# The dense stage of a two-layer kernel in batches of two steps: one power, one variance and one set of logits a batch

## The reference, cut

```python
# layer 0
c = lora(x, language) + embedding[language]
xq = act_fake_quant(c)                       # one scale over all of c
h = silu(xq @ Wgq.T) * (xq @ Wuq.T)          # 704 wide
x1 = x + act_fake_quant(h) @ Wdq.T           # one scale over all of h
# layer 1
a = relu(x1 @ W1[lang] + b1[lang]) @ W2[lang] + b2[lang]
z = x1 + a
n = (z - mean(z)) * rsqrt(var(z) + 1e-5) * gamma[lang] + beta[lang]
logits = n @ Wr                              # 9 experts
p = softmax(logits); w, e = top_k(p, 2); w = w / sum(w)
out = x1 + sum over the token's two experts of w * (silu(n @ Wg[e]) * (n @ Wu[e])) @ Wd[e]
```

## Time and profile before

| | us |
|---|---|
| median of 3 runs | 671.34 (667.01, 671.34, 673.58) |
| the profiled execution | 666.66 |
| its span | 664.9 |
| TensorE busy in the span | 604.4 (91%) |
| VectorE busy | 510.1 (77%) |
| ScalarE busy | 442.2 (67%) |
| GpSimd busy | 370.6 (56%) |
| mean granted clock of TensorE | 0.969 |

### The profile page before, as it was taken

The page is one execution under the profiler, slowest core; times in us unless marked ns, Lnnn a source line. Parts: engine busy times, 40 slices in busy tenths (PEclk is TensorE's granted clock), DMA queues, the critical chain, the costliest instruction groups (busy, mean ns, idle before and its releaser), DMA issues.

```text
span 664.9 us, 16051 instructions
## 1 busy us (share of the span) xinstructions
PE 604.4 (91%) x4404; PEld 412.9 (62%) x4404; DVE 510.1 (77%) x1373; ACT 442.2 (67%) x744; POOL 370.6 (56%) x573
## 2 busy tenths in 40 slices
PE   7988888898985558999999999999999999999994
PEld 2243335676663235777777777777777777777773
DVE  5589995688876879888988888888776666666652
ACT  3657995888864556888877787787665444445542
POOL 4014660047767683666657666667666555555544
PEclk9987999999998879999999999999999999999998
DMA  8524001256557649989899889866775556667552
GB/s 268 199 57 128 1 0 49 83 152 212 197 163 252 186 159 192 235 171 202 182 200 173 189 165 189 182 140 114 158 156 110 112 112 104 119 110 110 101 90 32
DMA packets 157300, 95.67 MB, mean 144 GB/s; under 512 B 107924, under 2 KB 150436, under 8 KB 157220
## 3 DMA queue, kind: packets, MB, share of 16 engines
q1 hardware_dynamic: 142900, 76.12, 47.7%
q0 software_dynamic: 13696, 18.51, 15.8%
q10 hardware_dynamic: 624, 0.03, 0.1%
HBM read 44.72 MB, written 24.68 MB: 104 GB/s over the span
## 4 chain that ended last, share of the span: by engine, by line
PE 55%; DVE 16%; issue 11%; POOL 6%; ACT 4%; DMA 3%; SPq 2%; another core or an unknown queue 1%; POOLq 1%; DVEq 0%; ACTq 0%
PE ps L692 29%; PE ps L743 15%; POOL rows L1643 3%; PE ps L564 2%; DVE big L1524 2%; PE ps L671 2%; DVE big L1364 2%; PE ps L803 1%; DMA small<-small 1%; DVE small L1189 1%; PE ps L582 1%; POOL small L1636 1%; PE ps L559 1%; DMA big<-in_low 1%
## 5 line engine op out<-in xcount | busy, mean ns | idle before, releaser
L692 PE MATMUL ps<-big,small 128*128 x1608 | 251.8, 313 | 2.8 <-ACT big L966 1.4
L692 PEld LDWEIGHTS ps<-big,small 128*128 128x128 f16 x1608 | 157.0, 98 | 81.3 <-issue 4.9
L1681 POOL DMA_INDIRECT out<-small x67 | 110.4, 1648 | 137.7 <-DVE small L1489 131.3
L743 PE MATMUL ps<-big,small 128*128 x1105 | 131.4, 273 | 0.5 <-DMA small<-small 0.5
L743 PEld LDWEIGHTS ps<-big,small 128*128 128x128 f16 x1105 | 105.3, 98 | 12.0 <-issue 0.6
L972 ACT ACTIVATE small<-small 128x704 f16<-128x704 f32 x67 | 52.6, 785 | 77.5 <-DVE small L1464 76.9
L1480 DVE SCALAR_TENSOR_TENSOR small<-small 128x64 f16<-128x64 f32 (+1 forms) x134 | 72.6, 583 | 19.9 <-ACT small L976 19.9
L1464 DVE SCALAR_TENSOR_TENSOR small<-ps,small 128x704 f32<-128x704 f32 x67 | 63.5, 948 | 24.9 <-PE ps L692 23.1
L976 ACT ACTIVATE small<-small 128x704 f16<-128x704 f32 x67 | 59.1, 882 | 28.0 <-DVE small L1474 28.0
L1643 POOL DMA_INDIRECT rows<-small x64 | 66.8, 1044 | 18.0 <-issue 18.0
L1654 POOL TENSOR_SCALAR small<-small 128x1 f32<-128x1 f32 x67 | 71.2, 1063 | 0.0
(11 more groups left out here) (256 smaller groups left out, 1048.7 us busy)
## 6 DMA issues: line engine op xcount, KB each, us to landing
small<-rows SPq DMA_DIRECT2D x67, 130.0 KB
big<-in_Wg SPq DMA_DIRECT2D x8, 704.0 KB, 4.6
big<-in_Wu SPq DMA_DIRECT2D x8, 704.0 KB
big<-in_Wd SPq DMA_DIRECT2D x8, 640.0 KB, 5.1
big<-in_xT SPq DMA_DIRECT2D x8, 512.0 KB, 7.1
small<-in_xT SPq DMA_DIRECT2D x16, 256.0 KB
out<-big SPq DMA_DIRECT2D x16, 256.0 KB
rows<-small SPq DMA_DIRECT2D x13, 130.0 KB, 4.2
```

The source lines that it names most:

```text
L692: m = e.matmul(ps[:, 2 * j + h, 0:352], xsT_(t)[:, 2 * xp + k, :], bigh[:, bass.ds(o + (4 * j + 2 * wp + k) * I + 352 * h, 352)], start=(n ...
L743: m = e.matmul(ps[:, 7, 0:H], hTE_(t)[:, hc_, :], bigh[:, bass.ds(o + 8 * I + (6 * wp + c) * H, H)], start=(n == 0), stop=(n == len(terms) ...
L1681: e.indirect_dma_start(out=out[:, :], out_offset=bass.IndirectOffsetOnAxis(ap=tok_(t), axis=0), in_=yw_(t), in_offset=None, compute_op=ALU ...
```

## The change

Every engine's loop over steps becomes a loop over batches, with two steps in a round, in a new order.

- `variance`, `power` and `logits` run once a batch on both steps; `mhalf`, `vpe`, `ssq` are used four columns wide, `rstd` has two buffers.
- `route` is cut in two functions, `first_choice` (up to `df`) and `second_choice`; a `clip_h` stands between.
- TensorE: the filler ahead of `rank` and inside `logits_and_rows` goes; three fillers stand ahead of each `adapter_in`. `adapter_out` of a batch's second step and the `rank` of two batches back stand between the dense products of the batch. `adapter_in` stands ahead of `logits_and_rows`.
- ScalarE: `relu` ahead of `evac_x1`, `squares` at the ends of a round.
- GpSimd: power, then all eight scatters of the batch two back.
- The residual waits for `px` too, as `logits_and_rows` now comes later than `adapter_in`.
- SP: `load_l1` stands behind the x load of its batch's first step; two stores of x1 come after the first two pieces of weights.
- VectorE: `order_experts` and `first_tiles` in the last round, between `residual(15)` and `logits` of batch 6. Behind the stage the last batches' work is ordered anew, and TensorE's `rank(last)` comes ahead of tile 0.

```diff
--- before.py
+++ after.py
@@ carving
-        mhalf = carve(small, a, [2])
+        mhalf = carve(small, a, [2, 2])
...
-        rstd = carve(small, a, [2, 2])
+        rstd = [carve(small, a, [2, 2]) for _ in range(2)]
@@ new helpers
+        def step(of, s):
+            if 0 <= s < ST:
+                of(s)
+
+        def batch(of, b):
+            if 0 <= b < NB:
+                of(b)
@@ sync
-            for i in range(2, 17):
-                if i < ST:
-                    load_xk(i)
+            for i in range(2, ST):
+                load_xk(i)
+                if i >= 6 and i % 2 == 0:
+                    load_l1(i // 2)
                 store_x1(i - 2)
-                b = (i - 5) // 2 + 3
-                if i >= 5 and i % 2 == 1 and b < NB:
-                    load_l1(b)
             load_piece(0)
             load_piece(1)
+            store_x1(ST - 2)
             store_x1(ST - 1)
@@ tensor, rank and logits_and_rows
-                if b < last:
-                    keep_busy(3, 6)
...
-                keep_busy(4 if s else 6, 2 + 2 * (s % 2))
@@ tensor, the stage
-            for i in range(1, 17):
-                if i == 2:
-                    dense_down(1)
-                if i >= 2:
-                    logits_and_rows(i - 2)
-                    adapter_in(i - 2)
-                if i <= ST and i != 2:
-                    dense_down(i - 1)
-                if i >= 2:
-                    adapter_out(i - 2)
-                if i >= 5 and i % 2 == 1:
-                    rank((i - 5) // 2)
-            logits_and_rows(ST - 1)
-            adapter_in(ST - 1)
-            adapter_out(ST - 1)
-            rank(6)
+            for b in range(NB + 1):
+                step(dense_down, 2 * b)
+                batch(rank, b - 2)
+                step(adapter_out, 2 * b - 1)
+                if 0 < b < NB:
+                    keep_busy(3, 1)
+                step(adapter_in, 2 * b)
+                step(dense_down, 2 * b + 1)
+                step(logits_and_rows, 2 * b)
+                if b < NB:
+                    keep_busy(3, 0)
+                step(adapter_in, 2 * b + 1)
+                step(logits_and_rows, 2 * b + 1)
+                step(adapter_out, 2 * b)
+            keep_busy(12, 0)
             piece_top(0)
+            keep_busy(6, 0)
             piece_top(1)
-            keep_busy(14, 0)
+            keep_busy(10, 0)
+            rank(last)
             turn_rows(0)
             proj(0, 0)
             proj(0, 1)
             turn_rows(1)
             piece_top(2)
-            rank(last)
@@ scalar, the stage
-            for i in range(18):
-                if i >= 4:
-                    squares(i - 4)
-                if i < ST:
-                    shift_h(i)
-                if i >= 2:
-                    evac_x1(i - 2)
-                    relu(i - 2)
-                if i % 2 == 1 and i < ST:
-                    adapter_gate(i // 2)
-                if EARLY <= i < ST:
-                    floor_h(i)
-                if i % 2 == 0 and 2 <= i < ST + 2:
-                    scale_beta(i // 2 - 1)
-                if i >= 5 and i % 2 == 1:
-                    second_weight((i - 5) // 2)
-            squares(ST - 2)
+            for b in range(-1, NB + 1):
+                step(squares, 2 * b - 1)
+                batch(second_weight, b - 2)
+                step(shift_h, 2 * b + 2)
+                step(relu, 2 * b)
+                if b >= 0:
+                    step(floor_h, 2 * b + 2)
+                batch(adapter_gate, b)
+                step(evac_x1, 2 * b)
+                step(relu, 2 * b + 1)
+                batch(scale_beta, b - 1)
+                step(shift_h, 2 * b + 3)
+                step(evac_x1, 2 * b + 1)
+                if b >= 0:
+                    step(floor_h, 2 * b + 3)
+                step(squares, 2 * b)
             piece_sum(0)
             piece_sum(1)
             piece_hi(0)
-            squares(ST - 1)
             x_hi(0)
+            second_weight(last)
@@ vector: residual, variance, route
+                w.wait_ge("px", s - 1)
...
-            def variance(s):
+            def variance(b):
+                w.wait_ge("sq", 2 * b + 2)
+                w.wait_ge("rstd", b)
+                e.tensor_scalar(vpe, ssq, eps2[:, 0:1], eps2[:, 1:2], ALU.mult, ALU.add).then_inc(S["vpe"], 1)
...
-            def route(b):
+            def first_choice(b):
...
+            def second_choice(b):
                 e.tensor_tensor(Eq, L2, bc(m2), ALU.is_equal).then_inc(S["rt"], 1)
@@ vector, the stage
-            for i in range(1, 18):
-                rb, odd = divmod(i - 5, 2)
-                if i == 2:
-                    clip_h(1)
-                if i >= 2:
-                    residual(i - 2)
-                if i <= ST and i != 2:
-                    clip_h(i - 1)
-                if i >= 4:
-                    variance(i - 4)
-                if i >= 5 and odd:
-                    positions(rb)
-                if i == 16:
-                    order_experts()
-                    first_tiles()
-                if i >= 3:
-                    gain(i - 3)
-                if i >= 4:
-                    logits(i - 4)
-                    affine(i - 4)
-                if i >= 5:
-                    (payload if odd else route)(rb)
-            variance(ST - 2)
-            positions(6)
-            gain(ST - 1)
-            logits(ST - 2)
-            affine(ST - 2)
-            piece_scale(0)
-            payload(6)
-            variance(ST - 1)
+            for b in range(-1, NB):
+                step(affine, 2 * b - 3)
+                step(residual, 2 * b)
+                step(gain, 2 * b - 1)
+                step(clip_h, 2 * b + 1)
+                batch(positions, b - 2)
+                batch(variance, b - 1)
+                batch(payload, b - 2)
+                step(affine, 2 * b - 4)
+                step(residual, 2 * b + 1)
+                if b == last:
+                    order_experts()
+                    first_tiles()
+                batch(logits, b - 1)
+                batch(first_choice, b - 1)
+                step(clip_h, 2 * b + 2)
+                batch(second_choice, b - 1)
+                step(gain, 2 * b)
+            affine(ST - 3)
+            gain(ST - 1)
+            positions(last - 1)
+            variance(last)
+            payload(last - 1)
+            affine(2 * last - 2)
+            piece_scale(0)
+            logits(last)
+            first_choice(last)
+            second_choice(last)
             piece_scale(1)
             x_lo(0)
             piece_lo(0, (0, 1))
             evac_rows(0)
-            logits(ST - 1)
-            affine(ST - 1)
             piece_lo(1, (0, 1))
             x_lo(1)
-            route(last)
-            piece_scale(2)
+            affine(ST - 1)
             positions(last)
             payload(last)
+            affine(ST - 2)
+            piece_scale(2)
@@ gpsimd
-                e.tensor_tensor(rstd[:, r, :], vpe[:, r, :], mhalf, ALU.pow).then_inc(S["rstd"], 1)
+                e.tensor_tensor(rstd[b % 2], vpe, mhalf, ALU.pow).then_inc(S["rstd"], 1)
...
-                w.wait_ge("aff", 2 * b + half + 1)
+                w.wait_ge("aff", 2 * b + 2 - half)
...
-            for i in range(4, 18):
-                power(i - 4)
-                b, half = divmod(i - 7, 2)
-                if i >= 7:
-                    scatter(b, half)
-            power(ST - 2)
-            scatter(5, 1)
-            power(ST - 1)
-            scatter(6, 0)
-            scatter(6, 1)
-            scatter(last, 0)
-            scatter(last, 1)
+            power(0)
+            for b in range(1, NB + 2):
+                batch(power, b)
+                if b >= 2:
+                    scatter(b - 2, 0)
+                    scatter(b - 2, 1)
```

36 lines of the change are left out of this document (16 added, 20 removed).

## The result

The changed kernel took 683.30 us (median of 4 runs, 682.18 to 687.06) against 670.82 for the kernel before (4 runs): a ratio of 1.0188, 95% interval 1.0139 to 1.0237. The forecast was 664.1, the range 657 to 677. Both were wrong, and so was the likeliest direction. The profiled execution took 684.10 us, its span 682.3 (664.9 before), the mean granted clock 0.949 (0.969).

A forecast was written before the change was run, and what follows sets the result against it. With no engine full, the prediction took a dense-stage step's loop, filler inside, as the bound. Batches -7.2, late signals +1.5 and hand-over -1.5 sum to -7.2 us, against the median 671.34: 664.1 us, range 657 to 677.

The forecast's parts named there:

- The batch: Dense stage, step 2's gain to step 14's: period falls from 12.30 to 11.1 us, six batches gain 7.2 us.
- the parameter wait that I had called covered: Dense stage: adapter wants parameters about 7.5 us after SP starts on them, some 12 now; any wait within late-signal bounds.
- The reading that the filler is on the loop: Dense stage: filler, 0.88 us, lies inside each step's loop; ScalarE's waits for TensorE are 1.74 us of a batch.
- The power on four columns: GpSimd, once a batch in place of two on two columns: 0.75 us, between 0.72 and 1.44.
- Late signals: Dense stage stalls, tied to SP's parameter loads, rise from some 2 to 3.5 us: 1.5 lost, between -2 and +5.5.
- A sign that I had named: Granted clock in the dense stage under 0.95 would show the prediction wrong in step one.
- The hand-over: Step 14's gain to tile 1's first products: 29.2 us becomes 27.7, 1.5 us gained, between 0 and 3.
- Tile 1 to the end: The part behind tile 1's first products was to take the same 430 us as now.
- B: Dense stage: with less filler TensorE's clock falls, a batch takes 14.3 us, 12 us slower, 683 us; chance 0.17.
- A: Dense stage: period stays at about 12 us, late scatters eat the hand-over's gain, 2 us remain, 669 us; chance 0.33.
- C: Dense stage and hand-over: no late signal and fast landings, -12.2 us, 659 us; chance 0.12.

The follow-up runs named there:

- e8: The kernel before with only the filler products of its batches removed, on a chip with signals on time: 657.46 us, ratio 0.9985 to the kernel before.
- c_after_3: The changed kernel, unchanged, run once more on a chip where TensorE's signals reach VectorE late: 680.18 us, one run.
- c_after: The changed kernel, unchanged, on a chip where TensorE's signals come on time: 657.92 us, ratio 1.0001 to the kernel before.
- c_before: The kernel before, unchanged, profiled on a chip where TensorE's signals come on time: 658.01 us, one run.

## Why the prediction was wrong, step by step

**The batch, -7.2 us: right in kind, too large.** With prompt signals the five batches from gain(2) on step by 11.2, 11.2, 12.2, 11.5 and 11.5 us, where the kernel before has 12.2 in each: 3.5 us gained, where five times 1.2 would be 6. Two things were missed. I took the trace's 12.30, a little of which was late signals (12.24 with prompt ones). And the batch of 12.2 has TensorE waiting 2.51 us for `in_bet` (the row above): the parameter wait that I had called covered, or at worst within the bounds. The reading that the filler is on the loop is borne out by e8, at a granted 1.00. The sixth batch gained 0.3 and not 1.2: its round is the long one in both kernels (13.4 and 13.7 us), as VectorE also orders the experts there, 2.4 us, and I had not set it apart. From 172.6 to 184.1 us VectorE runs without an idle row, as laid out. The power on four columns took 1.04 us, not 0.75; GpSimd had room for it.

**Late signals, +1.5 us (bounds -2 and +5.5): this is the step that failed.** In the first measurement the stretch from gain(2) to gain(14) has 89.7 us against 71.0 with prompt signals; the kernel before has 78.4 against 74.8. The change thus raised the price of late signals there from 3.6 to 18.7 us, 15.1 more, nearly three times my upper bound. (These are differences of single executions on different chips.) The rows were before me: the stalls marked "remote" in the earlier trace rows. I tied them to SP's parameter loads because SP was busy at the time, and scaled them by the number of such groups. Had I laid GpSimd's timeline beside them, the match would have shown: the first late signal of the kernel before, that of `dense_down(6)`, comes at 145.46 and a group of four scatters ends at 145.5. What the change does is to join two groups of four, with a power between them, into one of eight, 10.4 us long in a period of 11, and to put the dense product, the rank and `adapter_out`, for all of which VectorE waits at once, into it. The change's part that mattered most, the joining of the scatters, was one that I costed at nothing but GpSimd's time. A sign that I had named came too: the granted clock from 130 to 200 us is 0.88, under 0.95.

**The hand-over, -1.5 us (0 to -3): wrong sign.** +3.5 us in the first measurement, +4.9 with prompt signals (31.4 against 26.5). The path was the one described, and VectorE did wait over 5 us for `x_hi(1)` (6.2; prompt 7.1). The terms: I had the last scatter of batch 5 end 15.3 us after gain(14), it took 18.5 (215.95 - 197.48), because power(7) starts 5.3 and not 4.2 us behind it, takes 1.2 with its joint and not 0.9, and the eight scatters take 11.9 us, not 10.2. The rest, 12.9 us, is less than my 13.9. And the base was wrong: 29.2 held late signals, without them it is 26.5. A stall that I counted on losing was in the number that I compared with.

**Tile 1 to the end, 430 us:** 433.4 in the first measurement, where the last scatters still run until 256.5; 427.2 to 428.7 on the prompt chips.

**The rivals.** B gave 683, and the time was 683, but that is luck: B's mechanism is not what began the loss. (B's own sum was also off: with half of TensorE's work at half speed a batch is 9.8 x 1.5 = 14.7 us and not 14.3, which makes 686.) On prompt chips the changed kernel, with the same fillers, has a granted 1.00 up to 186 us:

```profile
120.00:142.00 22.00, 20.18 (x152) 15.78 (x152) 19.36 (x80) 20.59 (x40) 2.07 (x2) 1.00 0.37 111
142.00:186.00 44.00, 39.81 (x301) 31.12 (x300) 40.02 (x174) 39.81 (x73) 33.78 (x34) 1.00 0.65 194
```

c_after_3 has 0.88 in the second stretch. The clock falls behind TensorE's waits of 3.7 to 4.7 us and makes them dearer (1.85 for 1.10 us above); it does not begin them. But what B feared of less filler is real in e8, the kernel before without its fillers. The section of the Trainium skill that the prediction weighed ("TensorE: Matmul & The Clock Gate", "A second HAM failure mode: psum-queue depth-cycling") would have small repeated gaps swing the clock. The traces agree with it in part. c_after has gaps of 1.0, 1.1 and 2.5 us, one a batch in three batches up to 186 us (in the others two of 0.2 and 0.3 us), at a granted 1.00, and c_before one of 1.12 us in every batch, also at 1.00. e8 has three gaps a batch, of 0.2 to 1.8 us, and there the clock does swing. A was nearest in mechanism: late signals eat the period, late scatters the hand-over; its size, 669, was that of a period back at about 12 us, and from gain(6) on the batches took 14.9 to 18.2. C, no late signals, has its own chips: the result there was no change, not -12.
